# Token attention: the splits of weights and eight norms at other steps of VectorE's order

## What is computed

```python
def _attn_block(q_src, k_src, v_src, Wq, Wk, Wv, Wo, bo):      # 16 heads of 64
    q, k, v = split_heads(q_src @ Wq), split_heads(k_src @ Wk), split_heads(v_src @ Wv)
    attn = softmax(einsum('bhid,bhjd->bhij', q, k) * 64 ** -0.5)
    out = einsum('bhij,bhjd->bhid', attn, v)
    return merge_heads(out) @ Wo + bo
out = x1 + _attn_block(x1, x2, x2, Wq, Wk, Wv, Wo, bo)
return _attn_block(out, out, x1, Wq, Wk, Wv, Wo, bo)
```

## Time and profile before

| | |
|---|---|
| median of 3 runs | 2516.03 us (2514.41 to 2516.48) |
| the profiled execution | 2517.56 us |
| its span | 2515.8 us |
| TensorE (PE) matmuls busy | 2298.0 us, 91% |
| VectorE (DVE) busy | 1523.7 us, 61% |
| ScalarE (ACT) busy | 1103.0 us, 44% |
| GpSimd (POOL) busy | 1073.9 us, 43% |

### The profile page before, as it was taken

How to read it: one execution, slowest core, us unless ns; L and a number is a source line. 1 busy time by engine, 2 the same in 40 slices (tenths; PEclk the granted TensorE clock), 3 DMA queues, 4 the chain that set the end, 5 groups by cost and what they waited for, 6 DMA issues and landing times.

```text
span 2515.8 us, 34568 instructions
## 1 busy us (share of the span) xinstructions
PE 2298.0 (91%) x12918; PEld 1438.5 (57%) x12918; DVE 1523.7 (61%) x2281; ACT 1103.0 (44%) x2349; POOL 1073.9 (43%) x785
## 2 busy tenths in 40 slices
PE   6999999879988999999899998799899589989998
PEld 3333443357754555555555554588656467768887
DVE  6778678357745666663766666432444556656556
ACT  1667567623323444441344444133322457743233
POOL 2556547424444788873668888033401122100000
PEclk7899999999999999999999999899999699989999
DMA  6354433232110111112011111255210141010001
GB/s 127 117 95 94 82 62 69 65 77 40 1 18 1 14 14 15 10 34 35 2 14 15 14 10 18 69 134 134 31 55 22 51 117 51 1 59 17 1 1 34
DMA packets 138067, 114.50 MB, mean 46 GB/s; under 512 B 74823, under 2 KB 115253, under 8 KB 137517
## 3 DMA queue, kind: packets, MB, share of 16 engines
q1 hardware_dynamic: 100749, 111.36, 16.5%
q0 software_dynamic: 36864, 0.15, 4.3%
q10 hardware_dynamic: 288, 0.79, 0.2%
HBM read 86.26 MB, written 13.40 MB: 40 GB/s over the span
## 4 chain that ended last, share of the span: by engine, by line
PE 69%; DVE 12%; DMA 9%; ACT 3%; issue 3%; POOL 2%; SPq 2%; DVEq 0%; POOLq 0%; ACTq 0%
PE PS L120 66%; DMA adj<-e_EE,e_IX 7%; DVE c_MX L1784 2%; SPq L146 2%; DVE g_SS L124 1%; PE PS L1189 1%; DVE c_WS L124 1%; ACT a_P L839 1%; POOL c_AC L124 1%; DVE a_MX L733 1%; DVE g_st L1274 1%; PE PS L352 1%; DMA a_KS<-a_KL 1%; DVE X L396 1%; DMA a_r<-a_RQ 0%
## 5 line engine op out<-in xcount | busy, mean ns | idle before, releaser
L345 POOL DMA_INDIRECT adj<-e_EE,e_IX x256 | 414.4, 1619 | 460.9 <-DMA adj<-e_EE,e_IX 348.8
L124 POOL TENSOR_TENSOR c_AC<-c_AC,c_P 128x1024 f32<-128x1024 f32 x150 | 379.5, 2530 | 90.4 <-DVE c_AC L124 83.3
L1784 DVE TENSOR_REDUCE c_MX<-PS 128x2 f32<-128x1024 f32 x256 | 312.7, 1221 | 170.5 <-PE PS L120 170.5
L1881 ACT ACTIVATE c_P<-PS 128x1024 f32<-128x1024 f32 x256 | 250.9, 1026 | 237.9 <-PE PS L120 230.0
L733 DVE TENSOR_REDUCE a_MX<-PS 128x2 f32<-128x1024 f32 x256 | 303.4, 1219 | 59.2 <-PE PS L120 57.9
L839 ACT ACTIVATE a_P<-PS 128x512 f32<-128x512 f32 x512 | 270.5, 601 | 91.1 <-PE PS L120 90.2
L120 PE MATMUL PS<-c_P,c_VV 128*64 128x512 f32 x1024 | 247.7, 605 | 0.0
L129 POOL TENSOR_SCALAR e_EQ<-e_KR,e_KC 128x128 bf16<-128x128 f32 x256 | 162.8, 636 | 159.3 <-DMA e_KR<-adj_key 122.9
L120 PE MATMUL PS<-a_QS,a_KS 64*128 64x512 f32 x512 | 195.0, 463 | 16.2 <-ACT a_P L839 8.5
L120 PE MATMUL PS<-a_KS,a_QS 48*128 48x512 f32 x512 | 170.8, 475 | 12.0 <-DVE a_MX L733 4.9
L120 PEld LDWEIGHTS PS<-a_QS,a_KS 64*128 64x128 f32 x512 | 84.4, 190 | 169.0 <-ACT a_P L839 96.6
(11 more groups left out here) (499 smaller groups left out, 4620.3 us busy)
## 6 DMA issues: line engine op xcount, KB each, us to landing
e_KR<-adj_key SPq DMA_DIRECT2D x64, 256.0 KB, 3.7
f_W<-in_L_ffn_w SPq DMA_DIRECT2D x16, 1024.0 KB, 7.9
c_RB<-c_r SPq DMA_DIRECT2D x60, 128.0 KB, 2.9
g_FB<-in_fside_1x16xSxS SPq DMA_DIRECT2D x8, 616.0 KB, 8.0
a_QS<-a_QH SPq DMA_DIRECT2D x32, 128.0 KB, 3.9
adj<-e_zt SPq DMA_DIRECT2D x16, 256.0 KB, 4.2
adj<-e_EE,e_IX POOLq DMA_INDIRECT x256, 3.2
d_AJ<-adj SPq DMA_DIRECT2D x8, 512.0 KB, 7.6
```

Source lines behind the costliest of these rows:

```text
L124: return v.e.tensor_tensor(o, a, b, op)
L345: g.e.indirect_dma_start(self.adj, bass.IndirectOffsetOnAxis(ap=self.IXE[:, k:k + 1], axis=0), self.EE[:, k:k + 1], None, compute_op=ALU.a ...
L1784: v.e.reduce_max(MX[:, w % 2, :, qt, kh], bank(0, 2).rearrange("p (h n) -> p h n", h=2), AX, negate=True).then_inc(*smax_dve.up())
L1881: s.e.activation(PB[t % NP][:, :, :].rearrange("p h n -> p (h n)"), bank(2 + 2 * (t % 2), 2), ACT.Exp, scale=0.125).then_inc(*st_act.up())
```

## The change

Only the order of jobs is changed. In rounds 16 and 17 two norms each stand at steps 2 and 3, ahead of the additions of the step, in place of one at each even step behind them. In the 13 odd rounds the coarse casts stand at steps 2 (k) and 3 (q), and all four subtractions of "fine" at step 4, ahead of VectorE's second addition. No instruction is added or removed.

```diff
@@ -1535,22 +1535,28 @@
                     yield "st", w, n
                     if n == 5 and w + 1 < W:
                         yield "m", w + 1
+
+                    if w in (16, 17) and n in (2, 3):
+                        for t in range(2):
+                            yield "norm", 4 * (w - 16) + 2 * (n - 2) + t
+                    if w % 2 and w % 16 != 15 and w // 2 + 2 < 16:
+                        if n in (2, 3):
+                            yield "coarse", w // 2 + 2, 3 - n
+                        if n == 4:
+                            yield "fine", w // 2 + 2, 1
+                            yield "fine", w // 2 + 2, 0
                     if 3 <= n < lead(w) + 3:
                         yield "add", w, n - 3
                     if n - 1 > lead(w):
                         yield "acc", w, n - 1
                     if n == 0 and not first:
                         yield "acc", w - 1, 7
-                    if w in (16, 17) and n % 2 == 0:
-                        yield "norm", 4 * (w - 16) + n // 2
                     if w in (17, 18) and n % 2 == 0:
                         yield "turn", 4 * (w - 17) + n // 2
                     if n == 1 and not first and w - 2 >= 16 * b:
                         yield "recip", w - 2
                     if n == 4 and not first and w - 2 >= 16 * b:
                         yield "scale", w - 2
-                    if w % 2 and w % 16 != 15 and w // 2 + 2 < 16 and 2 < n < 7:
-                        yield ("coarse", "fine")[(n - 3) % 2], w // 2 + 2, n < 5
                     if n == 6 and w in (13, 15):
                         yield "fetch", w // 14
                     if n % 2 == 0:
```

## The result

| | before | after |
|---|---|---|
| median of 20 runs | 2519.32 us | 2511.07 us |
| the profiled execution | 2517.56 us | 2514.62 us |
| its span | 2515.8 us | 2512.8 us |

The ratio is 0.9968 (95% interval 0.9957 to 0.9980): 8.1 us faster, 5.0 to 10.8. Forecast were 13 us, 2503 us against a median of 2516.0 us.

What follows compares the result with a forecast made beforehand. TensorE, busy 91% of the span, was taken to wait for VectorE's maximum, held up by splits blocked behind GpSimd's add. Gains 12.0 + 0.3 + 0.9 = 13.2 us off 2516.0 gave 2503 us, range 2500 to 2510.

Steps and rivals of the forecast that it cites:

- Term 1: Splits of step 6 in odd rounds: moved to step 4, no longer blocked by GpSimd's add; 12.0 us gained over 11 rounds.
- Term 2: Step 4's added load on VectorE, ScalarE and GpSimd: cost 0 with thin cover; lower end leaves 8.8 us of the 12.0.
- Term 3: Norms moved in rounds 16 and 17: 0.3 us gained from exchanged TensorE waits, 0.9 us from the clock.
- clock step: TensorE's granted clock behind the waits of rounds 16 and 17: between 0 and 1.7 us gained, half taken, 0.9 us.
- The first rival: GpSimd loses its slack and blocks VectorE's first add, 0.3 to 0.8 us per pair; 2506 to 2512 us, chance 0.27.
- The second rival: The wait only moves: GpSimd's adds come over 2 us late each odd round; 2514.8 us, no change, chance 0.08.
- the third: VectorE's burst in step 4 becomes the bound through GpSimd's adds, exponentials waiting for them; 2531.7 us, slower, chance 0.03.

Runs made afterwards that it cites:

- the second trace: The changed kernel run and traced again, nothing altered; ratio to the kernel before 0.9975 (0.9960 to 0.9990).
- the splits alone: Against the kernel before: splits and casts moved as in the change, norms left at their old steps; 2499.72 us against 2516.74, ratio 0.9929.
- the one with two sends: Against the changed kernel: the send at step 3 removed, two sends a round in place of three; one run, 2500.92 us.
- the norms alone: Against the kernel before: norms moved as in the change, splits and casts left at their old steps; 9.1 us slower, ratio 1.0036.
- the splits behind the addition: Against the changed kernel: the four splits of step 4 put behind VectorE's second addition; ratio to the kernel before 1.0033.
- some sixty left: Splits moved, norms one each at step 0 of rounds 16 to 23, one send a round (step 5); 2602.98 us, ratio 1.033.

## Why the prediction was right or wrong

**Term 1 was right, mechanism and size.** Each pair of rounds won 1.07 us where nothing interfered (45.0 us before, 43.93 after), against 1.09 forecast: 11.8 us in 11 pairs, forecast 12.0.

**Term 2 was put at 0 and cost 1.8 us.** Five of the eleven pairs lost 0.33 to 0.37 us again, so S1 and S3 together won 5.7 + 4.2 = 9.8 us (10.3 in the second trace, where four pairs lost). That is the branch that the prediction had named and priced (0.3 us a pair) and had not taken, on a tie of 0.14 us between a send and the second addition: the tie went the other way in five rounds. Without that send the loss is gone. The rest of term 2 held: the copy and the next maximum had room, and the first addition of the even round took 2.84 us, forecast 2.9, without a wait of TensorE behind it.

**Term 3 failed at its clock step.** Forecast was a gain of 0.3 + 0.9 us, measured in S2 is a loss of 1.1 us. The waits themselves were worked out well: 2.33 and 2.99 us forecast, 2.21 and 3.26 measured. The clock step was wrong twice over: the wait of 2.33 us was given no fall at all, and that of 2.99 us only half of one, where both fell, against one before. S2 cut at the 18th and 19th transposition shows it, for the kernel before, the changed one, the splits alone and, in its first two parts, the one with two sends (columns as in the earlier trace rows):

```profile
1175.78:1217.32 41.54, 40.20 (x205) 32.11 (x204) 22.77 (x53) 9.52 (x14) 13.92 (x9) 1.00 0.20 26
1217.32:1241.05 23.73, 23.05 (x133) 11.72 (x132) 19.89 (x27) 11.15 (x17) 17.52 (x8) 1.00 0.07 2
1241.05:1272.03 30.98, 26.11 (x140) 12.85 (x138) 22.55 (x26) 11.98 (x18) 16.77 (x8) 0.94 0.08 10
```

```profile
1173.31:1218.69 45.38, 42.00 (x205) 32.92 (x204) 25.45 (x59) 9.65 (x14) 15.10 (x11) 0.96 0.17 24
1218.69:1246.34 27.65, 24.39 (x133) 12.54 (x131) 18.54 (x30) 11.33 (x18) 16.39 (x9) 0.94 0.05 1
1246.34:1270.69 24.35, 24.35 (x140) 12.20 (x138) 13.81 (x15) 11.60 (x16) 16.64 (x8) 1.00 0.11 12
```

```profile
1238.75:1263.10 24.35, 24.35 (x140) 12.08 (x138) 17.08 (x22) 11.61 (x16) 16.61 (x8) 1.00 0.11 12
```

```profile
1167.32:1211.14 43.82, 40.43 (x205) 31.68 (x204) 24.68 (x59) 9.44 (x14) 13.96 (x9) 1.00 0.16 24
1211.14:1238.29 27.15, 24.17 (x134) 12.27 (x132) 18.91 (x31) 11.44 (x19) 15.13 (x8) 0.94 0.04 1
```

The first part has the wait of round 16. With two sends there is no fall behind it and the part takes 43.82 us, with the fall 45.38: a fall cost 1.6 us here, close to the 1.7 us that term 3 had taken. Of the 2.3 us of error 1.5 are this fall, and 0.8 lie in the second part: a wait 0.3 us longer than forecast, and about the half of a fall that was not counted. What term 3 credited was right: the third part is 6.6 us shorter, forecast 4.96 + 1.7.

What the term doesn't show is to whom that credit belongs. The splits alone bring the third part to the same 24.35 us. With the splits already moved, the move of the norms therefore gains nothing and costs S2 97.38 - 89.62 = 7.8 us (11 us between the two medians). This changes nothing in the forecast of the whole, but half of the change was not worth making.

**The sum.** S1 to S3 bring 5.7 - 1.1 + 4.2 = 8.7 us in the first trace, 9.1 in the second, against 13.2 forecast, and the medians say 8.1 (5.0 to 10.8). The sign was right. The shortfall of 5 us alone would have stayed inside the range, which left room for 7. The range failed because it was also laid against a median of three runs, 2516.0 us, which is 3.3 us under that of twenty: 2502.8 + 5.0 + 3.3 gives the measured 2511.1, 1 us past the end of 2510. That the three runs came out low was bad luck; the two terms were not.

The first rival (part given back through GpSimd, 2506 to 2512 us) is the one that came true in the time, partly by luck. It had the loss through GpSimd in every pair, with at most 8.8 us left of term 1; it came in five of eleven, and 9.8 us were left. The time fits because the clock took 2.3 us that the rival did not have. The second rival did not happen, nor the third: no exponential waited for GpSimd in a regular round.

The lock is what the Trainium skill has, on the page SBUF — State Buffer, section Who interferes with whom: a VectorE instruction with two SBUF inputs contends with a GpSimd instruction that reads SBUF, and the shared ports are an exclusive lock; 2.43 us against 0.28 agree. Where the same section says that such an instruction did not stall the descriptors of GpSimd's transfers, the sends of 2.25 us behind an addition, against 1.56 elsewhere, still speak against it.

## What to carry to other kernels

Cost each half of a change against the kernel that has the other half already; a wait that two moved pieces stand in is won once. Here either half alone took it away or nearly so, and so the second half brought only its cost. Several small instructions that are harmless one by one are not when they stand in a row ahead of the one that TensorE waits for: count the cover once for the whole row, and price a fall of the clock behind each wait of 2 us or more: here waits of 1.0 us had none behind them, those of 2.1 to 2.2 us in rounds 16 and 31 had one in ten of fifteen cases, and those of 3.0 to 4.0 us in all eight. When an engine's order leaves no slack, a tie between two queues should be forecast as lost in part of the rounds. And lay a range against a median of many runs when it is only a few microseconds wide: three runs were 3.3 us off here.

## What the runs showed that I had not expected

The wait of about 2.2 us in round 16 had the clock fall behind it in the two traces of the changed kernel and with the norms alone. It had none with the splits behind the addition, nor with two sends, where the window 1208 to 1212 us has it at 1.00: at this length the same wait can go either way.

Some thirty sends could be left for the stages behind at no cost that shows, although the chain of waits of the kernel before runs through "adj" for 7% of the span; with some sixty left the kernel was 86 us slower than before. A chain that is followed back through the last releaser names what came last, and not how far something else stood behind it.

In S1 of the kernels with the splits moved and two sends TensorE has no idle time left, so the rounds themselves, 21.97 us each, are now its work.
